# Finding a mixture layer's selected tokens in two halves of four experts, and its expert loops written out

## The chip, the cores and the metric

One core of a Trainium2 chip runs the whole program. The metric is the time of one execution in device microseconds (us); the value quoted for a kernel is the median of its runs. The engines are TensorE (PE in the rows; its weight loads are PEld), VectorE (DVE), ScalarE (ACT), GpSimd (POOL) and the DMA queues that SyncE (SP) and GpSimd fill.

## The reference

A transformer block on x of 2 x 2048 tokens of 256 values: a modulated layer norm, attention with 16 heads, and a mixture of 8 experts in which every expert picks its 512 best tokens. What follows the attention is what matters here:

```
scores = softmax(xf @ gate_w.T)                    # 4096 tokens x 8 experts
vals, idx = top_k(scores.T, 512)                   # per expert
y = layernorm(xf[idx]) * ln_w + ln_b               # 512 tokens per expert
h = gelu(y @ fc1.T + b1)                           # 256 -> 1024
out = (h @ fc2.T + b2) * kept_score                # 1024 -> 256
xf = xf.at[idx].add(out)                           # tokens chosen twice get both
result = x + gb * xf
```

## The kernel before

The program runs in three blocks: projections, attention, and `mixture` (line 920 on), the only one that the change touches. All engines have their own instruction stream and wait for each other by semaphores. Tokens lie in 32 tiles of 128 (`NT`), two tiles are a pair.

`mixture` first makes the gate's scores and a normalised copy of the tokens (`normed`, in DRAM). VectorE then finds each expert's threshold by a search over the bits of the score (15 digits, L1398 to L1421), with small matmuls of TensorE between (L1184), and numbers the chosen tokens of each expert from 1 to 512 (`chosen`, L1439; 0 is not chosen). From here on:

- **Turn back.** TensorE transposes `chosen` (L1195), so that a column `c` stands for one tile and expert parity; then it multiplies three pairs of the base term, `gate_pair` (L1155 to L1168): four f32 matmuls per pair write gb * h into PSUM, and `add_base` (L1458) adds it to the residual on VectorE. Sixteen pairs in all; five PSUM buffers (`PB`) hold them.
- **Places and one-hots** on VectorE, L1442 to L1456: the place is split in a high part (16 values) and a low part (32 values). Sixteen compares of 256 columns make `high_hot` (L1448), one product of 4096 columns makes the first half of `token_of` (L1452, ScalarE makes the second at L1306), and 32 compares make `low_hot` (L1455). `onehot_done` counts to 3 when all are there.
- **Search** on TensorE, L1200 to L1206: 64 matmuls of 128x128 bf16, 32 tiles for each half `a` of the experts, add up, at (low, high), the row and the tile of the token that holds each place (`found_ps`).
- **Indices.** VectorE makes token numbers of them (L1467, L1468), four f32 matmuls spread these over the partitions (L1210), VectorE writes `idx_all` (L1472) and `sides` (L1475, L1476), which says to which batch a token belongs.
- **The other eleven base pairs** (L1213, L1477). SyncE stores the finished tiles of the result (L1085).
- **Experts.** GpSimd gathers an expert's 512 rows with four indirect DMAs (`gather`, L1531), two experts ahead; TensorE transposes them (`turn`, L1216), VectorE scales them into `yt` (`normed_in`, L1480), TensorE multiplies fc1 (L1229, waiting for ScalarE's gelu, L1312, to free one of two banks), transposes the next expert's rows, and multiplies fc2 (L1239); VectorE adds the bias and the kept weight (L1508, L1512), GpSimd adds the rows to the result (L1554). `over_experts` (L1035) runs experts 0 to 5 in a hardware loop of three rounds of two, with register values for the waits, and experts 6 and 7 behind it.

The order of the work on TensorE behind the one-hots is that of the program text:

```
pe.wait_ge(onehot_done, 3)
...  64 search matmuls, all experts
pe.wait_ge(tokens_done, 1)
...  4 matmuls that spread the indices
for p in range(PB, PAIRS): gate_pair(p)
pe.wait_ge(base_done, PAIRS)
turn(0, 0)
over_experts(pe, emit)
```

Of the kernel before, what the change touches and what calls it, by code (L numbers as in the profile page):

```python
# [22 lines left out]
P = 128  # L23
# [894 lines left out]
def mixture(nc, o):  # L918
# [22 lines left out]
    QE = P // LOW  # L941
    DIGITS = 15
    TRIES = 3

    with ExitStack() as st, nc.Block() as block:
# [11 lines left out]
        onehot_done, tokens_mm, tokens_done, idx_spread, idx_done = (  # L957
            sem("onehot_done"), sem("tokens_mm"), sem("tokens_done"), sem("idx_spread"), sem("idx_done"))
        ld_weights, gathered = [sem("ld_weights0"), sem("ld_weights1")], [sem("gathered0"), sem("gathered1")]
        ld_bias2 = [sem("ld_bias2_0"), sem("ld_bias2_1")]  # L960
# [13 lines left out]
        found_ps = bank[5][:, 0:2 * P].rearrange("p (a x) -> p a x", a=E // QE)  # L974
        spread_ps = bank[5][:, 2 * P:3 * P].rearrange("p (q a r) -> p q a r", q=QE, a=E // QE)
# [38 lines left out]
        idx_f = region_t[:, 3840:3840 + E * HIGH].rearrange("p (a q r) -> p a q r", q=QE, r=HIGH)  # L1014
        powers = st.enter_context(nc.sbuf_tensor("powers", [P, DIGITS, TRIES], I32))
# [19 lines left out]
        def over_experts(eng, emit):  # L1035

            with eng.Fori(0, E // 2 - 1) as n:
                emit(2 * n, n, 0, True, True)
                emit(2 * n + 1, n, 1, True, True)
            emit(E - 2, E // 2 - 1, 0, True, False)  # L1040
            emit(E - 1, E // 2 - 1, 1, False, False)

        def at(e, base=0):

            return bass.ds(e + base, 1) if not isinstance(e, int) else slice(e + base, e + base + 1)

        @block.sync
        def _(sp):
# [38 lines left out]
            with sp.Fori(0, E // 2 - 1) as i:  # L1087
                for j in range(2):

                    sp.wait_ge(sum_done, i * (2 * EC) + (2 + (j + 1) * EC))  # L1090
                    load(2 * i + (2 + j), j)
                    load_bias2(2 * i + (2 + j), j)
# [3 lines left out]
        def _(pe):  # L1096
# [112 lines left out]
            for q in range(QE):  # L1209
                last = nc.tensor.matmul(spread_ps[:, q, :, :], spread_ident[:, q, :, :].rearrange("p j l -> p (j l)"),  # L1210
                                        idx_f[:, :, q, :], start=True, stop=True)
# [388 lines left out]
```

## Time and profile before

| | |
|---|---|
| median of 3 runs | 1583.41 us (1582.59 to 1583.48) |
| the profiled execution | 1579.39 us |
| its span, first to last instruction | 1577.2 us |
| outside the span | 2.2 us |
| granted TensorE clock, mean | 0.959 of full speed |
| busy: TensorE, VectorE, ScalarE, GpSimd | 1459.4, 1194.4, 1080.2, 906.8 us |

Times within the trace are microseconds from the span's start. The attention ends and `mixture` begins near 1190; the places are ready at 1294, and the experts run from 1340 to 1570. A line such as L1204 is a line of the kernel before. In the chain of waits each piece follows from the one that released it.

### The profile page before, as it was taken

Reading aid. Unit: us, or ns where it says so; the run is one execution under the profiler, and the core shown is the slowest. Engines: PE = TensorE matmul, PEld = TensorE weight load, DVE = VectorE, ACT = ScalarE, POOL = GpSimd, SP = SyncE. Lnnn points to the kernel's source line nnn. Section 1 sums busy time; section 2 is a strip of 40 time slices with the busy share of each in tenths; the row PEclk is TensorE's granted clock in tenths of the full one; section 3 lists DMA queues with packets and bytes.
Section 4 is the critical chain, followed back from the end, with each engine's and each line's share of the span. In section 5 each row is a group of like instructions: output and inputs, shape, how many; then the busy total and the mean of one; then the engine's idle time right before and its main releaser. Section 6 shows DMA issues by size and latency. Waiting matters only on the chain. (4 is left out here: it accounts for less than half of the span.)

```text
span 1577.2 us, 43271 instructions
## 1 busy us (share of the span) xinstructions
PE 1459.4 (93%) x15923; PEld 1142.2 (72%) x16142; DVE 1194.4 (76%) x3650; ACT 1080.2 (68%) x2069; POOL 906.8 (57%) x1510
## 2 busy tenths in 40 slices
PE   6894999999999999999899999999997758999997
PEld 4551788888888888888788888888886546666675
DVE  6643999999999999999799999999976694223222
ACT  3443888898889888998788988898884770211211
POOL 3332777677767777777677777677773001324322
PEclk9997899999999999999999999999999856999999
DMA  6334222322232222223223222322234333334532
GB/s 219 121 118 147 70 64 63 91 72 67 61 91 75 67 62 78 83 71 109 66 67 94 71 64 63 92 74 65 88 126 142 93 114 122 99 95 98 153 74 24
DMA packets 90030, 142.44 MB, mean 90 GB/s; under 512 B 18032, under 2 KB 69632, under 8 KB 85728
## 3 DMA queue, kind: packets, MB, share of 16 engines
q1 hardware_dynamic: 82058, 128.70, 26.4%
q0 software_dynamic: 6464, 9.29, 3.2%
q8 instruction: 124, 2.03, 0.5%
q10 hardware_dynamic: 1302, 1.74, 0.3%
q14 instruction: 82, 0.67, 0.1%
HBM read 109.56 MB, written 30.15 MB: 89 GB/s over the span
## 5 line engine op out<-in xcount | busy, mean ns | idle before, releaser
L834 ACT ACTIVATE region_o<-turn_ps 128x512 f32<-128x512 f32 x576 | 347.5, 615 | 53.1 <-PE turn_ps L799 45.5
L788 PE MATMUL score_ps<-region_s 128*128 128x384 bf16 (+3 forms) x1061 | 347.3, 348 | 12.0 <-DVE maxima L867 4.9
L834 ACT ACTIVATE region_p<-turn_ps 128x512 f32<-128x512 f32 x512 | 304.7, 612 | 75.6 <-PE turn_ps L799 75.4
L799 PE MATMUL turn_ps<-ident,region_a 128*128 128x128 f32 x2048 | 335.6, 275 | 16.0 <-ACT region_o L834 4.8
L799 PE MATMUL turn_ps<-ident,region_x 128*128 128x128 f32 x2048 | 336.5, 274 | 1.7
L799 PEld LDWEIGHTS turn_ps<-ident,region_a 128*128 128x128 f32 x2048 | 260.0, 141 | 51.5 <-ACT region_o L834 13.6
L902 POOL TENSOR_SCALAR region_x<-region_x,maxima 128x1664 f32<-128x1664 f32 (+3 forms) x128 | 211.3, 1651 | 143.9 <-ACT region_x L839 140.7
L867 DVE CUSTOM_DVE_ANT_0 region_x<-score_ps,region_t,maxima 128x512 f32<-128x512 f32 (+1 forms) x416 | 272.2, 700 | 11.7 <-PE score_ps L788 10.6
L799 PEld LDWEIGHTS turn_ps<-ident,region_x 128*128 128x128 f32 x2048 | 254.4, 141 | 34.4 <-issue 6.5
L867 DVE CUSTOM_DVE_ANT_0 region_a<-score_ps,region_t,maxima 128x512 f32<-128x512 f32 (+1 forms) x352 | 231.4, 697 | 24.5 <-PE score_ps L788 22.9
L839 ACT ACTIVATE region_x<-region_x 128x512 f32<-128x512 f32 (+1 forms) x320 | 218.7, 684 | 4.5 <-DVE maxima L867 4.5
L902 POOL TENSOR_SCALAR region_a<-region_a,maxima 128x1152 f32<-128x1152 f32 (+4 forms) x160 | 183.5, 1147 | 12.1 <-POOL maxima L891 5.8
L1312 ACT ACTIVATE region_a<-bank,b_sb 128x512 f32<-128x512 f32 x64 | 44.0, 687 | 207.4 <-PE bank L1229 207.4
L788 PEld LDWEIGHTS score_ps<-region_s 128*128 128x128 bf16 x1280 | 122.9, 98 | 68.4 <-DVE maxima L867 35.4
L839 ACT ACTIVATE region_a<-region_a 128x512 f32<-128x512 f32 (+1 forms) x224 | 158.9, 710 | 3.9 <-DVE maxima L867 3.9
L814 PE MATMUL pv_ps<-region_o,vblock 128*32 128x128 f32 x4608 | 152.3, 275 | 0.7 <-ACT region_o L834 0.7
L867 DVE CUSTOM_DVE_ANT_0 region_a<-score_ps,region_t 128x384 f32<-128x384 f32 (+2 forms) x256 | 138.5, 550 | 18.2 <-PE score_ps L788 17.3
L814 PE MATMUL pv_ps<-region_p,vblock 128*32 128x128 f32 x4096 | 138.4, 276 | 0.0
L1554 POOL DMA_INDIRECT result<-region_a,idx_all x32 | 50.1, 1565 | 147.7 <-DVE region_a L1512 142.0
L814 PEld LDWEIGHTS pv_ps<-region_o,vblock 128*32 128x32 f32 x4608 | 118.0, 109 | 22.2 <-issue 15.9
L891 POOL TENSOR_SCALAR maxima<-maxima 128x1 f32<-128x1 f32 x352 | 76.3, 221 | 85.6 <-DVE maxima L867 85.6
L814 PEld LDWEIGHTS pv_ps<-region_p,vblock 128*32 128x32 f32 x4096 | 104.0, 109 | 26.4 <-issue 26.1
(215 smaller groups left out, 2163.3 us busy)
## 6 DMA issues: line engine op xcount, KB each, us to landing
region_t<-factor_rows SPq DMA_DIRECT2D x32, 1024.0 KB
region_x<-in_fc_t SPq DMA_DIRECT2D x16, 1024.0 KB, 8.5
region_s<-q_split SPq DMA_DIRECT2D x64, 192.0 KB
region_s<-k_split SPq DMA_DIRECT2D x64, 192.0 KB
q_split<-region_o SPq DMA_DIRECT2D x16, 384.0 KB, 2.7
k_split<-region_t SPq DMA_DIRECT2D x16, 384.0 KB, 2.6
heads_out<-region_o SPq DMA_DIRECT2D x254, 17.0 KB
region_x<-in_x SPq DMA_DIRECT2D x4, 1024.0 KB, 15.2
```

Source lines behind the costliest of these rows:

```text
L788: nc.tensor.matmul(score_ps[:, j % SB, 0:(hi - lo) * P], stacks[:, b, 0, t * P:(t + 1) * P], stacks[:, b, 1, lo * P:hi * P], start=True, s ...
L799: last = nc.tensor.transpose(turn_ps[:, (h * NR + j) % TB, q * P:(q + 1) * P], rows[t][:, k * P:(k + 1) * P], ident[:, :])
L814: last = nc.tensor.matmul(pv_ps[VW * q:VW * (q + 1), short, :], vblock[:, b, k, :], weight(r)[:, q * P:(q + 1) * P], start=(k == 0), stop= ...
L834: nc.scalar.activation(weight(j), turn_ps[:, (h * NR + j) % TB, :], ACT.Exp).then_inc(exp_done, 1)
L839: nc.scalar.activation(row, row, ACT.Relu).then_inc(relu_act, 1)
L867: nc.vector.tensor_tensor_reduce(out=rows[t][:, lo * P:hi * P], in0=score_ps[:, j % SB, 0:(hi - lo) * P], in1=factors[:, b, u0:u0 + (hi - ...
L891: nc.gpsimd.tensor_scalar(maxima[:, 4, n:n + 1], top(n), -1.0, 0.0, ALU.mult, ALU.add).then_inc(negated, 1)
L902: nc.gpsimd.tensor_scalar(row, row, maxima[:, 4, n:n + 1], 1.0, ALU.add, ALU.mult).then_inc(shifted_pool, 1)
L1312: nc.scalar.activation(hidden[:, f, :], fc1_ps[f % 2][:, :], ACT.Gelu_apprx_tanh, bias=b1_sb[:, at(e), f].rearrange("p o -> p o")).then_in ...
L1554: nc.gpsimd.indirect_dma_start(out, bass.IndirectOffsetOnAxis(ap=idx_all[:, e, c:c + 1], axis=0), o_sb[:, e % 2, c, :], None, compute_op=A ...
```

## The change

Four things change, all behind `places_done`; the columns of the one-hots are also laid out with the half of the experts outermost (`own(a)`, 32 columns per quarter `q`), so that a half is a slice.

1. One-hots are made in two halves `a` of four experts: each compare covers 128 columns (4 x 32) in place of 256, and there are 96 in place of 48; the products of 4096 columns become two of 2048, on VectorE and on ScalarE. Each half has its own semaphore.
2. The search of half 0 (32 matmuls) waits for half 0 alone. The search of half 1 waits for half 1; its first four tiles run, then the indices of half 0 are spread, then three tiles and one base pair take turns.
3. The indices of half 0 are made, spread and saved ahead of the eleven late `add_base`; those of half 1 are made behind them, spread behind the transposes of expert 0, and saved behind `normed_in(0, 0)`. GpSimd's `gather(4)` waits for them. Expert 0's transposes wait for each of its four gathers alone.
4. The hardware loops over the experts are gone: all eight are written out on every engine, with constants in the waits.

```diff
-        onehot_done, tokens_mm, tokens_done, idx_spread, idx_done = (
-            sem("onehot_done"), ...)
+        onehot_done = [sem("onehot_done0"), sem("onehot_done1")]
+        gathered_first = [sem(f"gathered_first{c}") for c in range(EC)]
...
-        found_ps = bank[5][:, 0:2 * P].rearrange("p (a x) -> p a x", a=E // QE)
-        spread_ps = bank[5][:, 2 * P:3 * P].rearrange("p (q a r) -> p q a r", q=QE, a=E // QE)
+        found_ps = [bank[i][:, 0:P].rearrange("p (q s r) -> p q s r", q=QE, s=2) for i in (5, 7)]
+        spread_ps = bank[6][:, P:2 * P].rearrange("p (a q r) -> p a q r", q=QE, a=QA)
...
-            pe.wait_ge(onehot_done, 3)
-            for a in range(E // QE):
-                for t in range(NT):
-                    c = t * (E // QE) + a
-                    last = nc.tensor.matmul(found_ps[:, a, :], ...)
-                last.then_inc(tokens_mm, 1)
-            pe.wait_ge(tokens_done, 1)
+            def find(a, t):
+                c = a * NT + t
+                last = nc.tensor.matmul(found_ps[a]..., start=(t == 0), stop=(t == NT - 1))
+                if t == NT - 1:
+                    last.then_inc(tokens_mm, 1)
+            def spread_indices(a):
+                pe.wait_ge(tokens_done, a + 1)
+                for q in range(QE):
+                    last = nc.tensor.matmul(spread_ps[:, a, q, :], ..., idx_f[:, a, q, :], start=True, stop=True)
+                last.then_inc(idx_spread, 1)
+            pe.wait_ge(onehot_done[0], 3)
+            for t in range(NT):
+                find(0, t)
+            pe.wait_ge(onehot_done[1], 3)
+            for t in range(4):
+                find(1, t)
             pe.wait_ge(scaled_ident, B * KC + QE)
-            for q in range(QE):
-                last = nc.tensor.matmul(spread_ps[:, q, :, :], ...)
-            last.then_inc(idx_spread, 1)
-            for p in range(PB, PAIRS):
+            spread_indices(0)
+            pair = PB
+            for t in range(4, NT):
+                find(1, t)
+                if t % 3 == 0 and pair < PAIRS:
+                    gate_pair(pair)
+                    pair += 1
+            for p in range(pair, PAIRS):
                 gate_pair(p)
...
+            def turn_first():
+                for c in range(EC):
+                    pe.wait_ge(gathered_first[c], 16)
+                    for k in range(KC):
+                        last = nc.tensor.transpose(y_ps[k][:, c * P:(c + 1) * P], y_sb[:, 0, c, k * P:(k + 1) * P], ident[:, :])
+                        if c == EC - 1:
+                            last.then_inc(y_turned, 1)
...
             pe.wait_ge(base_done, PAIRS)
-            turn(0, 0)
-            over_experts(pe, emit)
+            turn_first()
+            spread_indices(1)
+            for e in range(E):
+                expert(e)
...  ScalarE
-            act.wait_ge(high_done, 1)
-            nc.scalar.activation(token_of[:, 1, :, :, :]..., high_hot..., ACT.Identity, scale=row_f[:, :]).then_inc(onehot_done, 1)
+            for a in range(QA):
+                act.wait_ge(high_done, a + 1)
+                nc.scalar.activation(token_of[:, 1, :, :, own(a)], high_hot[:, :, :, own(a)], ACT.Identity,
+                                     scale=row_f[:, :]).then_inc(onehot_done[a], 1)
...  VectorE
-            for r in range(HIGH):
-                last = nc.vector.tensor_scalar(high_hot[:, r, :, :], high, float(r + 1), None, ALU.is_equal)
-            last.then_inc(high_done, 1)
-            ...
-            for r in range(LOW):
-                last = nc.vector.tensor_scalar(low_hot[:, :, r, :], low, float(r + 1), None, ALU.is_equal)
-            last.then_inc(onehot_done, 1)
+            for a in range(QA):
+                for r in range(HIGH):
+                    last = nc.vector.tensor_scalar(high_hot[:, r, :, own(a)], high[:, :, own(a)], float(r + 1), None, ALU.is_equal)
+                last.then_inc(high_done, 1)
+                dve.wait_ge(high_done, a + 1)
+                dve.wait_ge(row_copied, 2)
+                nc.vector.tensor_tensor(token_of[:, 0, :, :, own(a)], high_hot[:, :, :, own(a)],
+                                        tile_q[:, :, own(a)].unsqueeze(1).to_broadcast([P, HIGH, QE, NT]), ALU.mult).then_inc(onehot_done[a], 1)
+                for r in range(LOW):
+                    last = nc.vector.tensor_scalar(low_hot[:, :, r, own(a)], low[:, :, own(a)], float(r + 1), None, ALU.is_equal)
+                last.then_inc(onehot_done[a], 1)
...
+            indices(0)
+            save_indices(0)
             for p in range(PB, PAIRS):
                 add_base(p)
+            indices(1)
...
             normed_in(0, 0)
-            over_experts(dve, emit)
+            save_indices(1)
+            for e in range(E):
+                expert(e)
...  GpSimd
+                if e == QE:
+                    pool.wait_ge(idx_done, E)
```

On TensorE, behind the transposes of the places, the order was this (`bank` is PSUM; L1166 is a base pair, L1204 the search, L1210 the spread of the indices, L1220 the transposes of expert 0):

```order
L1195 MATMUL bank<-ident,region_p 128x128 x2
L1166 MATMUL bank<-vblock,region_a 128x128 x12
L1204 MATMUL bank<-region_s,region_o 128x128 x64
L1210 MATMUL bank<-region_t,vblock 128x32 x4
L1166 MATMUL bank<-vblock,region_a 128x128 x44
L1220 MATMUL bank<-ident,region_c 128x128 x8
L1037 UNCONDITIONAL_BRANCH
```

And it is now, with the lines of the changed kernel (L1168 the base pairs, L1212 the spread, L1238 the transposes of expert 0, L1256 its fc1):

```order
L1168 MATMUL bank<-vblock,region_a 128x128 x12
L1204 MATMUL bank<-region_s,region_o 128x128 x36
L1212 MATMUL bank<-region_t,vblock 128x16 x4
L1204 MATMUL bank<-region_s,region_o 128x128 x3
L1168 MATMUL bank<-vblock,region_a 128x128 x4
...
L1204 MATMUL bank<-region_s,region_o 128x128
L1168 MATMUL bank<-vblock,region_a 128x128 x8
L1238 MATMUL bank<-ident,region_c 128x128 x8
L1212 MATMUL bank<-region_t,vblock 128x16 x4
L1256 MATMUL bank<-region_a,region_x 128x512 x16
```

Three search matmuls and a pair of four stand in turns nine times, the last search matmul and two pairs behind them; the second spread has moved behind the transposes of expert 0.

On VectorE the same stretch was (L1448, L1452, L1455 the one-hots, L1461 `add_base`, L1467 on the indices):

```order
L1448 TENSOR_SCALAR region_t<-region_t 128x256 x16
L1452 TENSOR_TENSOR region_s<-region_t 128x4096
L1455 TENSOR_SCALAR region_o<-region_t 128x4x64 x32
L1461 TENSOR_TENSOR region_v<-region_v,bank 128x512 x5
L1467 TENSOR_SCALAR region_t<-bank 128x128
L1468 TENSOR_TENSOR region_t<-region_t,bank 128x128
L1472 CAST idx_all<-bank 32x4x2x4 x4
```

and is now (L1482, L1486, L1489 the one-hots, L1495 `add_base`, L1502 on the indices):

```order
L1482 TENSOR_SCALAR region_t<-region_t 128x4x32 x16
L1486 TENSOR_TENSOR region_s<-region_t 128x64x32
L1489 TENSOR_SCALAR region_o<-region_t 128x4x32 x32
L1482 TENSOR_SCALAR region_t<-region_t 128x4x32 x16
L1486 TENSOR_TENSOR region_s<-region_t 128x64x32
L1489 TENSOR_SCALAR region_o<-region_t 128x4x32 x32
L1495 TENSOR_TENSOR region_v<-region_v,bank 128x512 x5
L1502 TENSOR_SCALAR region_t<-bank 128x64
L1503 TENSOR_TENSOR region_t<-region_t,bank 128x64
L1510 CAST idx_all<-bank 32x16 x4
```

Both halves of the one-hots and the five early `add_base` stand ahead of the indices of half 0.

## Rows read from the trace of the kernel before

**Rows 1.** The page: busy time of the engines over the span.

```profile
PE 1459.4 (93%) x15923; PEld 1142.2 (72%) x16142; DVE 1194.4 (76%) x3650; ACT 1080.2 (68%) x2069; POOL 906.8 (57%) x1510
```

**Rows 2.** The chain that ended last: start, us, what, from the one-hots on.

```profile
1296.89 0.68 DVE region_t L1448 x5
...
1305.87 16.13 PE bank L1204 x64
...
1322.69 1.92 PE bank L1210 x8
1324.61 12.71 PE bank L1166 x88
...
1337.34 0.70 DVE region_v L1461
...
1338.09 0.67 PE bank L1220 x4
...
1340.45 15.69 PE bank L1229 x32
1356.14 0.87 PE bank L1220 x8
1357.01 13.81 PE bank L1239 x64
```

**Rows 3.** The same chain, expert 3.

```profile
1427.67 13.73 PE bank L1229 x32
```

**Rows 4.** Busy time by stretch; the column behind POOL is the granted TensorE clock.

```profile
1299.60:1303.00 3.40, 0.41 (x4) 0.21 (x2) 3.40 (x13) 3.38 (x2) 0.00 (x0) 1.00 0.01 2
1306.00:1322.00 16.00, 15.99 (x64) 11.09 (x64) 2.84 (x5) 0.00 (x0) 0.00 (x0) 0.50 0.20 67
1324.60:1330.00 5.40, 5.40 (x27) 5.40 (x27) 2.46 (x9) 0.00 (x0) 3.01 (x3) 0.50 0.33 97
1330.50:1337.30 6.80, 6.80 (x61) 6.61 (x60) 4.93 (x8) 0.00 (x0) 4.56 (x5) 1.00 0.88 261
1337.40:1340.40 3.00, 1.09 (x8) 0.86 (x8) 2.25 (x5) 0.00 (x0) 0.00 (x0) 1.00 1.06 374
1340.50:1343.90 3.40, 3.40 (x4) 1.36 (x5) 2.80 (x8) 0.00 (x0) 0.78 (x1) 0.51 0.47 164
1356.00:1570.00 214.00, 212.91 (x793) 145.47 (x791) 61.28 (x148) 39.17 (x57) 68.40 (x51) 1.00 0.38 94
```

**Rows 5.** VectorE in order of time: start, us, line, shape, [idle before].

```profile
1206.59 0.38 DVE L1358 BATCH_NORM_AGGREGATE region_t<-region_t 128x2 f32<-128x6 f32 x4
...
1299.19 2.29 DVE L1452 TENSOR_TENSOR region_s<-region_t 128x4096 bf16<-128x4096 bf16 x1
1301.40 4.42 DVE L1455 TENSOR_SCALAR region_o<-region_t 128x256 bf16<-128x256 bf16 x32
1305.73 3.11 DVE L1461 TENSOR_TENSOR region_v<-region_v,bank 128x512 f32<-128x512 f32 x5
1322.03 0.29 DVE L1467 TENSOR_SCALAR region_t<-bank 128x128 f32<-128x128 f32 x1 [13.19 <-PE bank L1204]
...
1328.22 0.69 DVE L1461 TENSOR_TENSOR region_v<-region_v,bank 128x512 f32<-128x512 f32 x1 [0.95 <-PE bank L1166]
1329.93 0.69 DVE L1461 TENSOR_TENSOR region_v<-region_v,bank 128x512 f32<-128x512 f32 x1 [1.02 <-PE bank L1166]
1331.09 0.69 DVE L1461 TENSOR_TENSOR region_v<-region_v,bank 128x512 f32<-128x512 f32 x1 [0.47 <-PE bank L1166]
1331.98 0.69 DVE L1461 TENSOR_TENSOR region_v<-region_v,bank 128x512 f32<-128x512 f32 x1 [0.21 <-PE bank L1166]
```

**Rows 6.** Who waited: TensorE for the one-hots.

```profile
PE bank L1204 <- DVE region_o L1455: 5.9, 1, 5.9
```

**Rows 7.** GpSimd: the first and fourth gather of expert 0, and the landing of all gathers.

```profile
1326.38 1.10 POOL L1537 DMA_INDIRECT region_c<-normed,idx_all  x1 [120.58 <-DVE idx_all L1472]
...
1330.31 0.95 POOL L1537 DMA_INDIRECT region_c<-normed,idx_all  x1 [0.30 <-issue]
...
DMA to landing us min/median/max: 3.5/5.1/6.6
```

**Rows 8.** ScalarE in order of time: its part of `token_of`.

```profile
1299.25 3.71 ACT L1306 ACTIVATE region_s<-region_t,row_f 128x4096 bf16<-128x4096 bf16 x1 [9.27 <-DVE region_t L1448]
```

More of the change, by code:

```diff
@@ L941, in mixture @@
     QE = P // LOW
+    QA = E // QE
     DIGITS = 15
@@ L1033, in tries, with gathered_all @@
             return slice(i % 2 * TRIES, (i % 2 + 1) * TRIES)
[L1035 to L1041, printed above, removed]
+        def gathered_all(eng, e):
+            if e == 0:
+                for c in range(EC):
+                    eng.wait_ge(gathered_first[c], 16)
+            else:
+                eng.wait_ge(gathered[e % 2], 16 * EC * ((e + 1) // 2))
         def at(e, base=0):
-            return bass.ds(e + base, 1) if not isinstance(e, int) else slice(e + base, e + base + 1)
+            return slice(e + base, e + base + 1)
         @block.sync
@@ L1085, in _ @@
                 sp.dma_start(out[t0 * P:t1 * P, :].rearrange("(t p) d -> p t d", p=P), xs[:, t0:t1, :]).then_inc(st_out, 16)
[L1087 to L1092, printed above, removed]
+            for e in range(2, E):
+                sp.wait_ge(sum_done, EC * (e - 1) + 2)
+                load(e, e % 2)
+                load_bias2(e, e % 2)
             sp.wait_ge(scattered, 16 * EC * E)
@@ new lines, in spread_indices @@
+            def spread_indices(a):
+                pe.wait_ge(tokens_done, a + 1)
+                for q in range(QE):
+                    last = nc.tensor.matmul(spread_ps[:, a, q, :], spread_ident[:, q, :, :].rearrange("p j l -> p (j l)"),
+                                            idx_f[:, a, q, :], start=True, stop=True)
+                last.then_inc(idx_spread, 1)
[3 more added lines that the diff above has]
+            pe.wait_ge(onehot_done[1], 3)
@@ L1218, in turn, with expert @@
+            def turn(e):
+                gathered_all(pe, e)
                 for k in range(KC):
                     for c in range(EC):
-                        last = nc.tensor.transpose(y_ps[k][:, c * P:(c + 1) * P], y_sb[:, i, c, k * P:(k + 1) * P], ident[:, :])
+                        last = nc.tensor.transpose(y_ps[k][:, c * P:(c + 1) * P], y_sb[:, e % 2, c, k * P:(k + 1) * P], ident[:, :])
                     last.then_inc(y_turned, 1)
-            def emit(e, n, i, ahead, gathers):
-                pe.wait_ge(ld_weights[i], n * 32 + 32)
+            def expert(e):
+                i = e % 2
+                pe.wait_ge(ld_weights[i], 32 * (e // 2 + 1))
@@ L1231, in emit @@
                     last.then_inc(fc1_mm, 1)
-                if ahead:
-                    turn(n + i, 1 - i)
+                if e + 1 < E:
+                    turn(e + 1)
                 for c in range(EC):
@@ L1484, in normed_in, with expert @@
                                             ALU.mult, ALU.add).then_inc(yt_done, 1)
-            def emit(e, n, i, ahead, gathers):
-                dve.wait_ge(gathered[i], n * (16 * EC) + 16 * EC)
+            def expert(e):
+                i = e % 2
+                gathered_all(dve, e)
                 for b in range(B):
@@ L1514, in _ @@
             normed_in(0, 0)
-            over_experts(dve, emit)
+            save_indices(1)
+            for e in range(E):
+                expert(e)
         @block.gpsimd
```

61 lines of the change are left out of this document (28 added, 33 removed).

## The prediction, made blind

> **What bounds the kernel now.** I read the busy times first. TensorE is busy for 93% of the span, no other engine for more than 76% [rows 1]; the change touches only what follows the places, so I went to the chain of waits behind that point. There the reader should see four pieces [rows 2]: VectorE makes one-hots from 1296.89 to 1305.8, then TensorE alone carries the chain: the search of 16.13 us, the spread of 1.92, the late base pairs of 12.71. After one add on VectorE, the transposes of expert 0 start at 1338.09, and its fc1 at 1340.45. From there the experts run without a gap: expert 0 takes 15.69 + 0.87 + 13.81 us, and a later fc1 takes 13.73 [rows 2, 3]; over 1356 to 1570 TensorE is busy for 212.91 of 214 us at full clock [rows 4]. So the experts' stage is bound by matmuls that the change does not touch, and **only the start of fc1 of expert 0 can move the end**. The sum below asks when it starts instead of 1340.45.
>
> Next, the granted clock by stretch, since the same pair costs two prices. It is 0.50 (1.2 GHz) through the whole search and the first pairs and 1.00 (2.4 GHz) from 1330.5 on [rows 4]. The adds of VectorE show the pace of the pairs: 1328.22 to 1329.93 is 1.71 us per pair at the low level, 1331.09 to 1331.98 is 0.89 us at the high one [rows 5]. The clock rose 5.7 us after the pairs began (1324.6 to about 1330.3), and did not rise in 16 us of search. The last view is who waited for whom: TensorE stood for 5.9 us until the one-hots were there [rows 6], and VectorE for 13.19 us until the search was done [rows 5]. These two idle times are what the change splits.
>
> **Step 1, the one-hots.** Thirty-two compares of 256 columns take 4.42 us, 0.135 us from start to start (4.42 less one tail of 0.22, over 31) [rows 5]. What does one of 128 columns cost? The trace has none. Bounds: it can't exceed 0.135, and four tiny operations of 6 columns take 0.38 us with a tail of 0.15, 0.077 from start to start [rows 5]. The columns are thus worth at most 0.06 of the 0.135, and half of them leave 0.105, midway between the two ends; I take that, and keep 0.077 to 0.135 for the range. A half then takes 16 x 0.105 + 1.17 (half of 2.29, and a little start-up) + 32 x 0.105 = 6.2 us. Half 0 is ready at 1296.89 + 6.2 = 1303.1, 2.75 us sooner than now, half 1 at 1309.3, 3.5 us later than now. ScalarE's product of 3.71 us [rows 8] halves too and ends in front of both. Against this edit speaks a rule of the Trainium skill ("VectorE: DVE Perf Modes", the section on the TRN2 errata): an operation on SBUF pays a fixed latency each time, so that many small tiles pay it for each and tiles of 512 elements or more are advised. The rows agree, since about 0.077 of 0.135 us is of that kind: VectorE gets 3.5 us more work, and the sum bears it. By that page's formula of 58 cycles and a quarter of the columns, a half compare would cost about 0.094 us, an estimate by the page, and the indices of half 0 would come about 1 us sooner than I say.
>
> **Step 2, the search of half 0.** A search matmul takes 16.13 / 64 = 0.252 us [rows 2]. From 1303.15, 32 take 8.1 us, to 1311.2; half 1 has been ready since 1309.3, and four more end at 1312.2. VectorE has five adds to make behind the one-hots (start to start 0.61 [rows 5]): 1309.3 + 3.05 = 1312.4, then the two index operations, at about 0.25 each: 1312.9. TensorE thus stands for 0.7 us and spreads the indices of half 0 at 1313.0. The four matmuls have 16 columns in place of 32; the price of eight pieces in the chain is 1.92 us, 0.24 per piece, about that of a search matmul with four times the columns, so columns do not set it and I keep 1.92 [rows 2]: 1314.9 (a floor of half of that for the range). Here the old order was at 1324.6. Expert 0's gathers, issued from 1326.38 now [rows 7], start near 1316.7; four at 1.3 us and a landing of at most 6.6 us [rows 7] put them at 1328, behind cover until 1333. That their wait is now per gather is worth nothing.
>
> **Step 3, what is left in turns.** 28 search matmuls and 11 pairs. At the low clock a turn of three and one costs 3 x 0.252 + 1.7 = 2.46 us. At the high clock a pair is 0.89; a search matmul at the high clock isn't in the trace: between 0.126 (all of it scales) and 0.252 (none does); I take 0.19, since weight loads are busy for only 11.09 of the search's 16 us [rows 4] and neither they nor the columns explain it alone. When does the clock rise? Pairs alone needed 5.7 us [rows 4]; mixed with work that left it low, hardly less, and perhaps never, which is a rival below. I take a little more than the row, 6.5 us, that is 2.64 turns. What remains is 8.36 pairs x 0.89 + 20.1 x 0.19 = 11.3 us. Together 17.8 us, to 1332.7. The old order would have needed 28 x 0.252 + 12.71 = 19.8 for the same.
>
> **Step 4, the start of the experts.** The last add and its wait cost 0.77 us as now (1337.32 to 1338.09) [rows 2]. From there to fc1 it takes 2.36 us now. Both marks of the transposes now come at their end, which costs VectorE's first scaling about 0.3 us more, and the second spread (1 to 1.9 us) runs on TensorE while VectorE scales, 1.5 us: 2.65. VectorE's index work for it lies under the transposes, and saving it comes behind the scaling, with fc2's first add 15 us away. fc1 of expert 0 starts at 1332.7 + 0.77 + 2.65 = **1336.1 instead of 1340.45: 4.3 us sooner**.
>
> **Step 5, loops written out.** I cost it at nothing: the chain shows matmul after matmul through the loop's rounds, with fc1 at 13.73 us and no step between [rows 3]. What covers it is TensorE's own work; with that gone only a register operation per wait would show. The late indices (half 1) are due at the gather of expert 4, some 55 us later.
>
> The sum on the profiled execution: 1579.39 - 4.3 = 1575.1. That execution stands 4.0 us under the median shown, 1583.41, and the change's own time should stand to its median likewise: 1583.41 - 4.3 = **1579.1 us**. About 0.2% (3.2 us) is what a measurement of this kernel can tell from no change.
>
> **Rivals.**
>
> *The clock does not rise in the turns, slower (8%).* In the old order the pairs stood alone and the clock rose; now each stands between search matmuls, and the search alone kept the clock at 0.50 for 16 us though TensorE was busy for 15.99 of them [rows 4]. The Trainium skill ("TensorE: Matmul & The Clock Gate", on what is happening) says that the gate follows how busy TensorE has been lately; by that alone the search would have run at the high level. The row says no: busy in the records is not enough. The price: 28 x 0.252 + 11 x 1.7 = 25.8 us, to 1340.7; then 0.77, transposes at the low clock of about 2 us and the scaling or the spread of 1.9 behind them: fc1 at 1345.4, 4.9 us later than now, 1588.3 us. Each us longer at the low clock costs 0.4 us (a turn of 2.46 against 0.89 + 0.57 = 1.46), so it turns slower from 17 us of low clock on. Against it: the pair is the longer part of every turn, and pairs alone did raise the clock.
>
> *Half compares cost as much as whole ones (15%).* At 0.135 a half takes 7.65 us, half 1 is ready at 1312.2, the indices of half 0 at 1315.8, and 2.9 of the 4.3 us are gone: 1582.0, no change. Were the mode of the compare lost too, with 128 columns at the pace of the f32 adds (0.61 us for 512 [rows 5]), a half compare would cost about 0.077 + 0.13 = 0.2 us and the kernel come out some 5 us slower; nothing in the shapes asks for it, 2% of the whole.
>
> *The clock stays up into fc1 (12%).* After the pairs, TensorE did 1.09 us of work in 3 us, and the clock fell at 1340.5 to 0.51 for 3.4 us [rows 4]; fc1 of expert 0 took 15.69 instead of 13.73 [rows 2, 3]. If the second spread, or another moment of the fall, avoids that, 2.0 us more are gained: 1577.1.
>
> *The written-out code is supplied late (5%).* A stop of TensorE of some 0.3 us per expert, 2.4 us in all, gives 1581.5: the gain shrinks to no measurable change.
>
> **The numbers.** The forecast's own case has 60%: unknown costs (compare, search at the high clock 1.3 us either way, the rise of the clock 1 us either way) put it at 1577 to 1582, a quarter of it within 0.2%. Faster: three quarters of 60 (45), the clock case (12), and a few of the others (4): 0.61. Same: 15, the rest of the 60, 4 of the 5 and little else: 0.29. Slower: the low clock and the lost mode: 0.10. The range leaves out the slow rival and the far end of luck: 1575.5 to 1583.5.
>
> **What would show it.** Right: the first search matmul 2.7 us sooner behind the one-hots, the first gather about 10 us sooner, nine turns that go from 2.5 to 1.5 us, and fc1 of expert 0 some 4 us sooner relative to the one-hots, with every expert at 28.4 us. Wrong: start to start of the small compares near 0.135; a granted clock of 0.50 until the last pair; a gap on TensorE ahead of the first spread of over 1 us; or idle time on TensorE between experts.

## The result and the profile after

The change runs in **1572.93 us** (median of 4 runs, 1572.01 to 1575.28) against 1583.0 for the kernel before (4 runs, 1581.69 to 1583.48). The ratio is 0.9942, with an interval of 0.9927 to 0.9957: 9.2 us faster (6.8 to 11.6), or 0.6%. The forecast was 4.3 us faster, with a range down to 1575.5: the direction was as said and the size was not.

The profiled execution took 1572.41 us, its span 1570.6. The page's busy times, against [rows 1]:

```profile
PE 1470.8 (94%) x16150; PEld 1140.3 (73%) x16150; DVE 1199.0 (76%) x3707; ACT 1080.3 (69%) x2070; POOL 907.4 (58%) x1510
```

The chain of waits from the one-hots to the first experts, against [rows 2] (start, us, what; L1482, L1486, L1489 are the one-hots, L1495 the base add, L1212 the spread, L1204 the search, L1168 a base pair, L1238 the transposes of expert 0, L1256 its fc1):

```profile
1296.00 0.55 DVE region_t L1482 x5
...
1297.76 1.23 DVE region_s L1486
1298.98 3.26 DVE region_o L1489 x32
...
1305.14 3.27 DVE region_o L1489 x32
1308.40 3.07 DVE region_v L1495 x5
...
1312.00 1.86 PE bank L1212 x8
1313.86 0.75 PE bank L1204 x3
1314.61 1.71 PE bank L1168 x8
...
1321.15 0.89 PE bank L1168 x8
1322.04 0.74 PE bank L1204 x3
...
1330.37 1.80 PE bank L1168 x16
1332.19 0.70 DVE region_v L1495
...
1332.93 1.09 PE bank L1238 x8
1334.03 0.80 PE bank L1212 x8
1334.83 0.76 issue
1335.59 13.97 PE bank L1256 x32
1349.56 0.87 PE bank L1246 x8
1350.43 13.82 PE bank L1266 x64
```

VectorE makes both halves and five adds without a gap, and from the first spread on TensorE carries the chain. A turn of three search matmuls and one base pair takes 0.67 + 1.71 us at the low clock and 0.74 + 0.89 us at the high one. From the first one-hot to fc1 of expert 0 it takes 1335.59 - 1296.00 = 39.6 us, where the profile before has 43.6 [rows 2]. Behind that there is a second gain: fc1 of expert 0 takes 13.97 us and not 15.69. The clock by stretch, against [rows 4] (busy us of PE, PEld, DVE, ACT, POOL, then the granted clock):

```profile
1302.40:1311.60 9.20, 9.20 (x36) 6.20 (x36) 9.17 (x54) 3.49 (x3) 0.00 (x0) 0.50 0.11 37
1312.10:1319.40 7.30, 7.30 (x34) 6.80 (x35) 2.28 (x8) 0.00 (x0) 3.02 (x3) 0.50 0.46 147
1319.60:1332.10 12.50, 12.50 (x91) 11.41 (x89) 5.43 (x8) 0.00 (x0) 4.64 (x5) 1.00 0.71 218
1332.20:1335.50 3.30, 1.90 (x16) 1.80 (x16) 2.57 (x6) 0.00 (x0) 0.00 (x0) 1.00 0.82 280
1335.60:1349.50 13.90, 13.90 (x33) 6.20 (x34) 3.81 (x15) 4.81 (x7) 3.80 (x4) 1.00 0.15 39
```

The clock rises to 1.00 (2.4 GHz) inside the turns, near 1319.5, and stays there through the gap of 3.4 us and through fc1.

Between two single executions the span also holds chance differences from elsewhere (the first one-hot itself came 0.9 us earlier here). So from here on I use two lengths that hold only what the change can touch: **stretch**, first one-hot to fc1 of expert 0, and **experts**, from there to the last fc2. Their sum is 43.56 + 228.46 = 272.0 us before and 39.59 + 226.74 = 266.3 us after: 5.7 us, of which fc1's clock is 1.7. The runs differ by 9 to 10. The profile pair does not explain the result, and that was the first question.

### The profile page after: what moved, and what is told of

Same layout as the page of the kernel before. It is cut to its first block and busy times, and to the rows that moved or that the text cites. A ratio compares the mean times of both kernels' runs of the same rounds, so it can differ in the third digit from the quotient of the medians.

```text
span 1570.6 us, 43234 instructions
## 1 busy us (share of the span) xinstructions
PE 1470.8 (94%) x16150; PEld 1140.3 (73%) x16150; DVE 1199.0 (76%) x3707; ACT 1080.3 (69%) x2070; POOL 907.4 (58%) x1510
## 5 line engine op out<-in xcount | busy, mean ns | idle before, releaser
L788 PE MATMUL score_ps<-region_s 128*128 128x512 bf16 (+3 forms) x1280 | 406.1, 354 | 13.2 <-DVE maxima L867 8.9
L867 DVE CUSTOM_DVE_ANT_0 region_x<-score_ps,region_t,maxima 128x512 f32<-128x512 f32 (+1 forms) x416 | 272.0, 700 | 10.8 <-PE score_ps L788 9.9
L814 PEld LDWEIGHTS pv_ps<-region_p,vblock 128*32 128x32 f32 x4096 | 104.0, 109 | 26.1 <-issue 25.8
```

What stands on the lines that cost most here:

```text
L788: nc.tensor.matmul(score_ps[:, j % SB, 0:(hi - lo) * P], stacks[:, b, 0, t * P:(t + 1) * P], stacks[:, b, 1, lo * P:hi * P], start=True, s ...
L814: last = nc.tensor.matmul(pv_ps[VW * q:VW * (q + 1), short, :], vblock[:, b, k, :], weight(r)[:, q * P:(q + 1) * P], start=(k == 0), stop= ...
L867: nc.vector.tensor_tensor_reduce(out=rows[t][:, lo * P:hi * P], in0=score_ps[:, j % SB, 0:(hi - lo) * P], in1=factors[:, b, u0:u0 + (hi - ...
```

## The experiments

In each, times are medians of runs on one chip beside runs of the kernel before on that chip, whose median stands in the head of the table. Stretch and experts come from one profile of each kernel.

**Before and change again, loops apart.** Does the written-out code, which I costed at nothing, carry the rest? One kernel is the one before with this edit (and the like for SyncE's loads), another is the change with the opposite one and with one semaphore for the gathers of expert 0, as before:

```diff
-            with eng.Fori(0, E // 2 - 1) as n:
-                emit(2 * n, n, 0, True, True)
-                emit(2 * n + 1, n, 1, True, True)
-            emit(E - 2, E // 2 - 1, 0, True, False)
-            emit(E - 1, E // 2 - 1, 1, False, False)
+            for e in range(E):
+                emit(e, e // 2, e % 2, e + 1 < E, e + 2 < E)
```

> The kernel before, unchanged, profiled a second time with its timed runs. The profiled execution of before (1579.4 us, span 1577.2) lay 3.6 us under the median of its runs (1583.0), that of the changed kernel 0.5 us under its own. If the low one was luck of the TensorE clock, this profile lands near 1583 and the trace shows where the 3 to 4 us are: theory C expects them as stretches at the low clock (a mean granted clock under 0.959) before or in the first expert. Theory L (hardware loops) expects them inside the experts' stage: a round of the loop longer than 2 x 28.4 us.

> The kernel before with part 4 alone: experts' programs written out, nothing else. My prediction's step 5 gives 0 (ratio 0.9995 to 1.0005). Theory L, that the loops cost what the profile of before did not show, gives -3 to -5 us (1578 to 1580 against 1583).

> The changed kernel with the hardware loops put back (and one semaphore for expert 0's gathers as before). If the loops cost nothing: as the changed kernel, 1573. Theory L: 3 to 5 us more, 1576 to 1578. With theory C, fc1 of expert 0 starts about 40 us behind the one-hots' start either way and the clock at its start decides 2 us.

> The changed kernel, unchanged, on the same chip as the three others: 1572 to 1575, ratio 0.994. A second profile of it tells whether the clock stays up into fc1 again (13.97 us instead of 15.69).

| kernel (before: 1582.82) | median us | ratio, interval | stretch | experts |
|---|---|---|---|---|
| before | 1581.58 | 0.9993, 0.9982 to 1.0005 | 47.02 | 228.49 |
| before, written out | 1581.49 | 0.9991, 0.9982 to 1.0001 | 45.95 | 229.14 |
| change with loops | 1574.53 | 0.9943, 0.9928 to 0.9957 | 39.58 | 226.77 |
| change | 1572.80 | 0.9936, 0.9920 to 0.9953 | 39.53 | 226.74 |

The loops are worth nothing that the runs can tell. But the new profile of the *unchanged* kernel has a stretch 3.5 us longer than the one I predicted from. VectorE in that profile, from the fourth late add on, and GpSimd beside it (start, us, line, shape, [idle before]):

```profile
1330.58 0.69 DVE L1461 TENSOR_TENSOR region_v<-region_v,bank 128x512 f32<-128x512 f32 x1 [0.49 <-issue]
1331.58 0.69 DVE L1461 TENSOR_TENSOR region_v<-region_v,bank 128x512 f32<-128x512 f32 x1 [0.31 <-PE bank L1166]
1334.46 0.69 DVE L1461 TENSOR_TENSOR region_v<-region_v,bank 128x512 f32<-128x512 f32 x1 [2.20 <-PE bank L1166]
1337.31 3.08 DVE L1461 TENSOR_TENSOR region_v<-region_v,bank 128x512 f32<-128x512 f32 x5 [2.15 <-PE bank L1166]
```

```profile
1325.85 1.10 POOL L1537 DMA_INDIRECT region_c<-normed,idx_all  x1 [119.68 <-DVE idx_all L1472]
...
1334.78 0.95 POOL L1537 DMA_INDIRECT region_c<-normed,idx_all  x1 [0.30 <-issue]
```

And TensorE:

```profile
1329.79 7.05 PE L1166 MATMUL bank<-vblock,region_a 128*128 128x128 f32 x58
1337.28 0.59 PE L1166 MATMUL bank<-vblock,region_a 128*128 128x128 f32 x3 [0.44 <-issue]
1340.44 1.97 PE L1220 MATMUL bank<-ident,region_c 128*128 128x128 f32 x8 [2.57 <-DVE region_v L1461]
```

The trace puts VectorE's two idle times of 2.2 us down to TensorE, though TensorE ran pairs through them at 0.89 us each. What comes late is TensorE's signal. An add waits for the semaphore that the last matmul of its pair raises, and the trace also holds the moment of each raise. For the last six late pairs of this profile (us from the span's start):

| late pair | its last matmul ends | semaphore raised | add starts |
|---|---|---|---|
| 6 | 1332.32 | 1334.44 | 1334.46 |
| 7 | 1333.22 | 1337.28 | 1337.31 |
| 8 | 1334.11 | 1337.38 | 1337.91 |
| 9 | 1335.00 | 1337.47 | 1338.51 |
| 10 | 1335.90 | 1337.56 | 1339.11 |
| 11 | 1337.87 | 1337.88 | 1339.70 |

In the profile that I predicted from, each of the eleven raises comes 0.01 to 0.02 us behind its matmul. Here five come 1.7 to 4.1 us behind it, four of them within 0.3 us. VectorE starts 0.02 to 0.03 us behind the raise that it waits for, so VectorE is not what is held. The four pairs were not still to be multiplied either, since a pair takes 0.89 us. Whether the signal alone is held or the last part of the matmul too, whose end is modelled in the records, they don't tell; TensorE itself stood for 0.44 us inside its last pair, up to the moment of those four raises. The wait ends 1.6 us after the last gather's issue (1335.73 to 1337.31). Then VectorE makes the last five adds in one go, and TensorE waits 2.57 us for them. From here on a **stop** is such a wait of VectorE's late adds for a late signal. In the written-out kernel the chain itself shows one, and can't name who ended it, since no matmul ends at 1336.04:

```profile
1332.49 0.69 DVE region_v L1455
1333.18 2.86 another core or an unknown queue
...
1336.07 2.49 DVE region_v L1455 x4
```

Here too it ends 1.6 us after the last gather's issue (1334.51). In the profile that I predicted from, eight gathers were issued in the same place and no add stopped. Whether that execution was lucky or ran on a chip of another kind, which a later batch brings up, its record doesn't say: it names no chip, and the profiled time, 1579.39 us, is not among the timed runs beside it. **Theory: the kernel before usually pays for stops of VectorE's late adds beside GpSimd's gathers, and the change hides them. Rival: the stops go with SyncE's stores of the result, which run at the same time.**

**Stores or gathers.** Two variants of the kernel before: one holds back the stores, one the second expert's gathers, until all base adds are made. Two variants of the change, on the same chip, take out a part each: no turns (search of half 1 first, then all pairs), and one-hots of all experts made at once.

```diff
-                sp.wait_ge(base_done, 2 * g + 2)
+                sp.wait_ge(base_done, PAIRS)
```

```diff
             gather(0)
+            pool.wait_ge(base_done, PAIRS)
             gather(1)
```

```diff
             for t in range(4, NT):
                 find(1, t)
-                if t % 3 == 0 and pair < PAIRS:
-                    gate_pair(pair)
-                    pair += 1
-            for p in range(pair, PAIRS):
+            for p in range(PB, PAIRS):
                 gate_pair(p)
```

```diff
-            for a in range(QA):
-                for r in range(HIGH):
-                    last = nc.vector.tensor_scalar(high_hot[:, r, :, own(a)], ...)
+            for r in range(HIGH):
+                last = nc.vector.tensor_scalar(high_hot[:, r, :, :], high, ...)
...
-            pe.wait_ge(onehot_done[1], 3)
```

> Kernel before with SyncE's eight stores of the result held back until the last base add. In two of three profiles of before, VectorE's late adds stood still for 2 to 3 us at a time with the pair already multiplied, while GpSimd issued gathers and the DMA engines were nearly full; from the first one-hot to fc1 of expert 0 those two took 47.0 and 46.0 us, the third, without such stops, 43.6. If DMA traffic of the stores stops the adds: 43 to 44 us and no idle add. If GpSimd's gathers do it: as before, stops of 1 to 3 us between 1330 and 1338, 45 to 47 us.

> Kernel before with the four gathers of expert 1 held back until the last base add; those of expert 0 stay. If the issue of gathers on GpSimd stops VectorE's adds: no stop later than about 1 us behind the fourth gather (1332), and 43 to 45 us from the first one-hot to fc1. If the stores do it: stops up to 1337 as before, 45 to 47 us.

> The change with the 28 late search matmuls all ahead of the eleven pairs; halves, indices and written-out experts stay. Theory T (the turns raise TensorE's clock sooner and give VectorE slack against its stops): 2 to 5 us slower than the change, 42 to 45 us from first one-hot to fc1 against 39.6. Rival (only the earlier one-hots count, turns are worth nothing): 39 to 41 us.

> The change with the one-hots of all experts made at once as before (48 compares of 256 columns, one product), search, indices and turns as in the change. By my sum the search starts 3.1 us later behind the first one-hot (9.0 instead of 6.3) but the five early adds end sooner; the indices of half 0 then come at search end. From first one-hot to fc1: 39.6 + 2.7 = 42.3 us. Rival: TensorE was held at the indices of half 0 anyway, so less than 1 us.

| kernel (before: 1583.29) | median us | ratio, interval | stretch | experts |
|---|---|---|---|---|
| before, stores held back | 1583.35 | 0.9997, 0.9986 to 1.0007 | 46.19 | 228.99 |
| before, gathers of expert 1 held back | 1577.78 | 0.9963, 0.9949 to 0.9977 | 43.53 | 228.46 |
| change, no turns | 1574.43 | 0.9944, 0.9923 to 0.9965 | 39.20 | 226.74 |
| change, whole one-hots | 1575.38 | 0.9942, 0.9921 to 0.9963 | 40.89 | 226.74 |

The stores are not it: with them held back the chain has a stop of 2.13 us all the same, which ends at 1340.18, again 1.6 us after the last gather's issue:

```profile
1337.36 0.69 DVE region_v L1461
1338.05 2.13 another core or an unknown queue
...
1340.21 2.49 DVE region_v L1461 x4
```

One added wait on GpSimd takes 5.5 us off the kernel before, so a cost of the kernel before hangs on these four gathers. Not all of the 5.5 us can be read from rows: the one profile of this variant, the slowest of its five runs, is 3.2 us shorter in the two lengths (272.0 against 275.2) and has fc1 at 15.69 us. A later profile of the same kernel, on another chip, has fc1 at 14.0 us, so the clock may carry some of the rest. The whole one-hots lengthen the stretch by 1.3 us, not by the 2.7 that the later start of the search suggests; the runs can't tell that from nothing. The turns are worth nothing that the runs can tell.

**What holds the clock into fc1, and what is left in the change.** Second spread moved into expert 0 (it then stands inside fc1's time); the same four matmuls, their result unused, put behind the transposes in the kernel before with late gathers; expert 0's transposes put ahead of the last pair and its add; and the late gathers in the change.

```diff
             turn_first()
-            spread_indices(1)
...
+                if e == 0:
+                    spread_indices(1)
```

```diff
             turn(0, 0)
+            for q in range(QE):
+                nc.tensor.matmul(spread_ps[:, q, :, :], spread_ident[...], idx_f[:, :, q, :], start=True, stop=True)
             over_experts(pe, emit)
```

```diff
-            for p in range(pair, PAIRS):
-                gate_pair(p)
+            gate_pair(pair)
...
-            pe.wait_ge(base_done, PAIRS)
+            pe.wait_ge(base_done, PAIRS - 2)
             turn_first()
+            gate_pair(PAIRS - 1)
             spread_indices(1)
+            pe.wait_ge(base_done, PAIRS)
...  VectorE
             normed_in(0, 0)
+            add_base(PAIRS - 1)
             save_indices(1)
```

> The change with the second spread of indices (four small matmuls, 0.8 us) moved from ahead of fc1 of expert 0 to behind it. In all five profiles with that spread ahead of fc1 the clock stayed up and fc1 took 13.97 us; in all five profiles with the old order it fell and fc1 took 15.7 to 16.4 us. Theory S (the spread's work on TensorE keeps the clock up): fc1 15.7 us or more, 1.7 to 2.4 us slower. Rival (the shorter way from the last pair to fc1, or the moment of the fall): 13.7 to 14.0 us.

> The kernel of e6 (before, gathers of expert 1 held back) with the four spread matmuls repeated behind the transposes of expert 0, their result unused. Theory S: fc1 of expert 0 goes from 15.69 to about 14 us and the kernel gains 1.7 us on e6 (1576). Rival: 15.7 us, as e6, 1578.

> The change with the transposes of expert 0 put ahead of the last base pair and that pair's add behind normed_in(0, 0), so that VectorE scales while TensorE multiplies the last pair. By my sum fc1 starts 1.2 us sooner: 38.4 instead of 39.6 us from the first one-hot; the time 1571.7 against 1572.9. If the clock falls because the transposes now come before the pair, 13.97 becomes 15.7 and it loses 0.5 us.

> The change with the gathers of expert 1 held back until the last base add. If VectorE's stops beside the gathers are covered by the turns: 0 (39.5 us from one-hot to fc1, 1573). If they still cost: 1 us or more less. It also tells whether the gathers of expert 1 can wait in the change.

| kernel (before: 1582.19) | median us | ratio, interval | stretch | experts |
|---|---|---|---|---|
| change, second spread later | 1572.53 | 0.9945, 0.9926 to 0.9964 | 39.44 | 227.58 |
| before, late gathers, filler | 1577.02 | 0.9970, 0.9959 to 0.9982 | 42.13 | 226.77 |
| change, early transposes | 1572.92 | 0.9941, 0.9925 to 0.9956 | 38.34 | 226.77 |
| change, late gathers | 1573.45 | 0.9945, 0.9926 to 0.9964 | 39.47 | 226.74 |

Without the second spread the clock stays up as well (fc1 13.97), so the spread does not hold it. The late gathers, worth 5 us in the kernel before, are worth nothing in the change that the runs can tell: such a cost is not left in it. That is not because its adds never stop. In the profile after they do (VectorE; the fourth and fifth late adds behind the indices):

```profile
1322.62 0.69 DVE L1495 TENSOR_TENSOR region_v<-region_v,bank 128x512 f32<-128x512 f32 x1 [1.48 <-PE bank L1168]
1325.51 0.69 DVE L1495 TENSOR_TENSOR region_v<-region_v,bank 128x512 f32<-128x512 f32 x1 [2.20 <-PE bank L1168]
```

That is 2.89 us from start to start where the turns come every 1.63. Here too the signals are late: the pair ends at 1322.04 and 1323.67, the semaphore is raised at 1322.59 and 1325.48. In the profile of the change with the second spread later, one idle time is longer still, 3.60 us:

```profile
1325.91 2.50 DVE L1496 TENSOR_TENSOR region_v<-region_v,bank 128x512 f32<-128x512 f32 x4 [3.60 <-PE bank L1168]
```

But a turn gives VectorE 0.9 us of slack, the gathers start 10 us earlier behind the first one-hot (19.6 us against 29.5), and by the last pair VectorE has caught up. The early transposes shorten the stretch by 1.25 us, and the runs can't tell that kernel from the change.

**Issue, landing or GpSimd's arithmetic.** Kernels on the base of "gathers of expert 1 held back": that one again, and with, in the place of those gathers, four additions of 1024 columns on GpSimd; with four plain copies of as many rows by SyncE; with four gathers of 8 values per row (same issue, a thirty-second of the bytes). Results of the additions, copies and small gathers are not used.

```diff
             gather(0)
+            for c in range(EC):
+                nc.gpsimd.indirect_dma_start(small_rows[:, c, :], None, ..., IndirectOffsetOnAxis(ap=idx_all[:, 1, c:c + 1], axis=0)).then_inc(small, 16)
             pool.wait_ge(base_done, PAIRS)
+            pool.wait_ge(small, 16 * EC)
             gather(1)
```

> The kernel of e6 again as the reference of this batch (before, gathers of expert 1 held back until the last base add): 1577 to 1578, about 5 us under before, no stop of an add; fc1 of expert 0 15.7 us if the clock falls ahead of it, 14.0 if not.

> As f1, and where the gathers of expert 1 stood GpSimd adds 1024 columns four times on unused SBUF. If any work of GpSimd on SBUF stops VectorE's adds: stops between 1332 and 1338 as in before, 1581 to 1583. If it takes gathers: as f1.

> As f1, and SyncE copies 512 rows of the same length from DRAM into expert 1's buffer by four plain DMAs about when its gathers would land; GpSimd issues nothing then. If landing rows stop the adds: stops, 1581 to 1583. If the issue on GpSimd does: as f1, 1577 to 1578.

> As f1, and four gathers with expert 1's indices are issued where they stood, but of rows of 32 bytes into a small buffer (result unused): same issue on GpSimd, little to land. If the issue stops the adds: stops as in before, 1581 to 1583. If the landing of 1056-byte rows does: as f1.

| kernel (before: 1576.40, 31 runs) | median us | ratio, interval | stretch | experts |
|---|---|---|---|---|
| gathers of expert 1 held back | 1577.51 | 1.0006, 0.9993 to 1.0020 | 41.94 | 226.77 |
| + GpSimd additions | 1577.84 | 1.0006, 0.9993 to 1.0019 | 43.51 | 228.46 |
| + plain copies | 1576.35 | 0.9997, 0.9985 to 1.0009 | 41.99 | 226.77 |
| + small gathers | 1577.77 | 1.0005, 0.9990 to 1.0019 | 42.02 | 226.77 |

This batch can't answer its question, since the cost was not there: on this chip the *unchanged* kernel runs in 1576.40 us, 6 to 7 us under the three chips before, and holding back gathers gains nothing. No signal of TensorE is late in these four profiles, not even beside the four small gathers. So the cost seems to belong to some chips; the unchanged kernel itself was not profiled on a chip of this second kind. That gives a forecast for the change itself, tried on one more chip together with the small gathers:

> The changed kernel once more, on whatever chip this is. Where before runs at 1582 to 1583 (its adds stop): ratio 0.994, 1572 to 1573. Where before runs at 1576 to 1577 (they don't): 2.5 to 5.7 us by the profiles (0.9965 to 0.9985), because the change itself is at 39.5 us from one-hot to fc1 on both kinds.

> The kernel of f4 (before; four gathers of 32-byte rows where the gathers of expert 1 stood, the real ones behind the last add). On a chip where before runs at 1582 to 1583: if the issue on GpSimd stops VectorE's adds, as before, ratio 1.000; if the landing of full rows does, ratio 0.9965. On the other kind of chip: 1.000 either way, and it tells nothing.

| kernel (before: 1576.39, 23 runs) | median us | ratio, interval | stretch | experts |
|---|---|---|---|---|
| change | 1573.18 | 0.9979, 0.9970 to 0.9988 | 39.57 | 226.74 |
| + small gathers, on the kernel before | 1577.29 | 1.0004, 0.9996 to 1.0013 | 42.73 | 226.77 |

This chip is of the second kind too. The change takes the same time as in the other comparisons (1572.80, 1572.93, now 1573.18); only the kernel before differs. **The gain is 3.3 us (1.9 to 4.7) on a chip of the second kind, and some 9 to 10 on one of the first.** And in the change's profile on this chip, with all eight full gathers beside the late adds, no late add is late: each signal comes 0.01 to 0.02 us behind its matmul. The same two adds as above:

```profile
1323.41 0.69 DVE L1495 TENSOR_TENSOR region_v<-region_v,bank 128x512 f32<-128x512 f32 x1 [0.94 <-PE bank L1168]
1325.04 0.70 DVE L1495 TENSOR_TENSOR region_v<-region_v,bank 128x512 f32<-128x512 f32 x1 [0.94 <-PE bank L1168]
```

The profiles fall into the same two kinds. In all twelve from the three chips of 1582 to 1583 us, and in the profile after, some signal of TensorE is more than 0.3 us late or missing from the record; in the six from the two chips of 1576.4 us none is. In the profile that I predicted from, none is either: it looks like one of the second kind, where 1579.39 us is a usual time (the runs of the kernel before there lie between 1572.6 and 1581.1).

## Why the prediction was wrong, by its steps

The steps on the stretch held, in the profile after:

| step | predicted | measured |
|---|---|---|
| 1, half compare, start to start | 0.105 us | 0.103 (3.35 less a tail, over 31) |
| 2, first one-hot to first spread | 16.1 us | 16.0 |
| 2, first spread | 1.92 us | 1.86 |
| 3, clock rises, from the start of the turns | 6.5 us | 5.6 |
| 3, search matmul at the high clock | 0.19 us | 0.245 |
| 3, turns and remaining pairs | 17.8 us | 18.3 |
| 4, last pair to fc1 | 3.42 us | 3.42 |
| stretch | 39.2 us | 39.6 |
| 5, loops | 0 | 0 |

*Step 1.* By the formula of the Trainium skill ("VectorE: DVE Perf Modes", the section on the TRN2 errata) a half compare would have cost an estimated 0.094 us; the trace says 0.103. The part of a compare that does not shrink with its columns costs VectorE 3.5 us, and VectorE, with the two halves and then the five early adds, is what TensorE waits for ahead of the first spread. So the halves are worth only 1.3 us of the stretch, by one profile. *Step 2* is where most of the gain of the stretch seems to lie: the indices of half 0 are spread 9.8 us earlier behind the first one-hot (16.0 against 25.8), and half of the search moves behind them into the time of the late pairs. No kernel here tests that by itself. *Step 3* had two errors that partly cancelled: the clock rose 0.9 us sooner, and a search matmul at the high clock cost 0.245 us and not 0.19. The turns (the place of the first rival) are neither needed nor harmful by the runs of the kernel without them. *Step 5* stands: written out or not, both kernels show the same.

*The rival of the clock in fc1* (12%) happened, in all profiles of the change and its variants: fc1 of expert 0 takes 13.97 to 14.00 us, 1.7 us less than the 15.69 of the profile before. Two reasons can be excluded, the second spread and the filler: the kernel before with late gathers and no filler has 14.00 as well. In the kernel before and its variants, where the clock rose at most 4.0 us after the start of the first late pair and VectorE's adds ran without a long stop, it stayed up in fc1 (five profiles); where it rose after 5.6 to 5.8 us it fell (four); with an early rise and a long stop it fell too (two). So it goes with the timing; why, these runs don't tell.

**The step that failed** is the sentence under the sum, that the profiled execution "stands 4.0 us under the median shown, 1583.41, and the change's own time should stand to its median likewise". I took those 4.0 us for an offset common to both kernels. They were largely a cost of the kernel before that its median carries and its profiled execution lacks: the change's profiled execution stands 0.5 us under its median. The stops are that cost, and no row of the profile shows it. Whether the profiled execution lacked them by luck or by its chip is open. Counted by stretch and experts:

- before, three profiled executions on chips of 1582 to 1583 us (one of them written out, one with late stores): 275.5, 275.1 and 275.2 us, with stops; the one that I predicted from, without them: 272.0;
- late gathers in the kernel before: 268.7 to 272.0 us;
- the change and its kernels with the same order: 266.2 to 266.4 us.

From 275.2 to 266.3 is 8.9 us, against 9.2 by the runs: 4.0 us of stretch, which is the forecast's own mechanism (4.3), 1.7 us of clock in fc1, which was a rival, and 3.2 us of stops, a term that the forecast didn't have. From the 268.7 to 272.0 without stops it is 2.4 to 5.7, against 3.3 by the runs on the chip that has none. Both results thus come out of the same numbers. The forecast of 4.3 us lies within the interval of the second kind of chip, but no profile of the unchanged kernel on such a chip shows how its 3.3 us divide.

What is shown: the stops exist, VectorE waits in them for signals of TensorE that come up to 4.8 us late, and holding back expert 1's gathers takes about 5 us off the kernel before on two chips (on one of them with the filler), while holding back the stores takes off nothing that the runs can tell. What is only read from times and profiles: that they depend on the chip (three chips against two), and that they end 1.6 us after the last issue of a gather (three profiles of the old order; 1.4 us in the change without turns). What stays open: whether the issue on GpSimd or the arrival of the rows holds up the signals, by what way, and why a chip has it or not. The kernels that were to separate these ran on two chips without the stops.

## What to carry to other kernels

Before a sum is made against a profiled execution, ask why it is faster or slower than the median, and whether it ran on the chip of the timed runs. A difference of 4 us is as large as the forecast effect, and it need not pass to the changed kernel: one more profile of the unchanged kernel showed in one view what the first had hidden. When an engine stands idle though its input looks ready, compare the moment at which the semaphore was raised with the end of the work and with the start of the waiter: it tells which of the two sides is late. Where short VectorE operations wait for TensorE beside GpSimd's gathers, this kernel had idle times of 1 to 3.6 us on some chips: give them slack or move the gathers, and time the gain on more than one chip. And work that is moved forward pays only up to the next engine in line: half one-hots started the search 2.7 us earlier and shortened the stretch by 1.3.

## What was not expected of the hardware

- **TensorE's signals come late beside gathers, on some chips.** While GpSimd issues gathers and their rows arrive, the semaphore of a finished base pair is raised up to 4.8 us behind its last matmul (1335.42 and 1340.18 us in the kernel with late stores), and several raises then come about 0.1 us apart; the traces of three chips show such waits. The Trainium skill ("SBUF — State Buffer", on who interferes with whom) says that a VectorE instruction with at most one input in SBUF does not contend with GpSimd. These adds read one operand from SBUF and one from PSUM, and the traces agree with that sentence: an add starts 0.02 to 0.03 us behind the signal that it waits for and takes 0.69 us, in a stop as elsewhere. Nothing here shows what holds the signals.
- **The chip decides 0.4% of the same kernel.** The kernel before ran in 1582.2 to 1583.3 us on three chips and in 1576.4 on two others, with 14 to 31 runs each, while the change ran in 1572.8 us on one of the first and 1573.2 on one of the second.
- **A search matmul costs the same at both clocks.** 0.252 us at 1.2 GHz, 0.245 at 2.4 GHz (0.74 for three in a turn), while a base pair halves from 1.71 to 0.89 us. The rows don't say what sets it; the program reads the search's weights with a stride, which no run here varies.
